# An evacuation moved ahead of the sum of the probabilities in the first stage's bodies

## What is computed

```
q = conv3x3(x, wq) + bq;  k = conv3x3(x, wk) + bk;  v = conv3x3(x, wv) + bv
bias = conv7x7(x, wb) + bb
attn = einsum('bchw,bcjw->bchj', q, k) / 16 + bias
a = softmax(attn, axis=1)                 # over the 32 channels
out = einsum('bchw,bcjw->bchj', v, a)
x = x + out
```

## Time and profile before

| | before |
|---|---|
| median of 3 runs | 1191.78 us (1188.15 to 1192.03) |
| the profiled execution: its own time | 1191.42 us |
| its span, first to last instruction | 1189.6 us |
| PE busy | 1088.5 us, 92% |
| DVE busy | 803.9 us, 68% |
| ACT busy | 536.9 us, 45% |
| POOL busy | 322.7 us, 27% |
| the line of the first stage's convolutions (L1515) on the chain that ended last | 27% |
| one turn of the loop (from 168 us on) | 73 us |

### The profile page before, as it was taken

How to read it: one execution, slowest core, us unless ns; L and a number is a source line. 1 busy time by engine, 2 the same in 40 slices (tenths; PEclk the granted TensorE clock), 3 DMA queues, 4 the chain that set the end, 5 groups by cost and what they waited for, 6 DMA issues and landing times.

```text
span 1189.6 us, 38670 instructions
## 1 busy us (share of the span) xinstructions
PE 1088.5 (92%) x17124; PEld 792.3 (67%) x17124; DVE 803.9 (68%) x994; ACT 536.9 (45%) x747; POOL 322.7 (27%) x364
## 2 busy tenths in 40 slices
PE   2999999999999999999983689887989999999997
PEld 2999999999999899999951245332434444444443
DVE  6546585685757857477297978689988645466444
ACT  3524736546364563635345857677931212111110
POOL 1374546535464363545410000023300000000000
PEclk9999999999999999999995879989999999999999
DMA  6020020200202010010002445323354654566551
GB/s 211 7 77 4 3 77 3 77 3 3 77 3 77 3 30 16 3 42 3 3 2 54 94 99 129 75 63 74 93 140 131 193 168 107 173 173 192 155 141 41
DMA packets 52116, 89.79 MB, mean 75 GB/s; under 512 B 8795, under 2 KB 36699, under 8 KB 50940
## 3 DMA queue, kind: packets, MB, share of 16 engines
q1 hardware_dynamic: 44264, 80.56, 24.5%
q10 hardware_dynamic: 7700, 6.89, 2.0%
HBM read 36.89 MB, written 11.99 MB: 41 GB/s over the span
## 4 chain that ended last, share of the span: by engine, by line
PE 62%; DVE 22%; ACT 6%; issue 4%; SPq 2%; DMA 2%; DVEq 0%; ACTq 0%
PE psum L1515 27%; PE psum L1768 15%; PE psum L1779 10%; PE psum L1668 4%; DVE small L705 3%; DVE small L672 2%; DMA arena<-arena 2%; PE psum L1570 2%; ACT arena L1206 1%; DVE arena L625 1%; DVE small L586 1%; DVE arena L1004 1%; DVE small L665 1%; DVE psum L664 1%; DVE arena L677 1%
## 5 line engine op out<-in xcount | busy, mean ns | idle before, releaser
L1515 PE MATMUL psum<-arena 128*128 128x64 f16 (+2 forms) x11904 | 511.2, 206 | 24.1 <-DMA arena<-arena 12.6
L1515 PEld LDWEIGHTS psum<-arena 128*128 128x128 f16 x11904 | 493.7, 98 | 39.9 <-DVE arena L625 13.3
L625 DVE TENSOR_TENSOR arena<-psum,arena 128x512 f32<-128x512 f32 x128 | 87.8, 690 | 169.6 <-PE psum L1515 138.4
L1768 PE MATMUL psum<-arena 128*128 128x512 f16 (+2 forms) x936 | 191.5, 365 | 0.0
L1768 PEld LDWEIGHTS psum<-arena 128*128 128x128 f16 x936 | 91.9, 98 | 98.0 <-issue 2.3
L1427 POOL TENSOR_SCALAR arena<-arena,constants_f 128x256 f16<-128x256 f16 x126 | 138.6, 1128 | 0.0
L1423 POOL TENSOR_TENSOR arena<-arena 128x256 f16<-128x256 f32 x63 | 51.4, 816 | 305.7 <-ACT arena L1185 305.7
L1779 PE MATMUL psum<-arena 120*128 120x512 f16 (+1 forms) x528 | 116.9, 379 | 0.4 <-DMA arena<-edge_columns 0.4
L1180 ACT ACTIVATE arena<-arena 128x256 f16<-128x256 f32 x63 | 26.1, 415 | 188.3 <-issue 105.3
L1779 PEld LDWEIGHTS psum<-arena 120*128 120x128 f16 (+1 forms) x528 | 51.3, 97 | 62.5 <-issue 0.9
L1471 POOL TENSOR_TENSOR arena<-arena 128x1024 f32<-128x1024 f32 x16 | 30.4, 1898 | 207.5 <-ACT arena L1327 154.6
(11 more groups left out here) (211 smaller groups left out, 1434.3 us busy)
## 6 DMA issues: line engine op xcount, KB each, us to landing
arena<-in_filter_tables SPq DMA_DIRECT2D x8, 1280.0 KB, 8.6
arena<-arena SPq DMA_DIRECT2D x32, 264.0 KB, 3.9
X<-in_x SPq DMA_DIRECT2D x16, 512.0 KB, 4.8
arena<-arena SPq DMA_DIRECT2D x32, 256.0 KB, 3.9
out<-X SPq DMA_DIRECT2D x16, 512.0 KB, 4.0
arena<-edge_columns SPq DMA_DIRECT2D x90, 80.0 KB
arena<-edge_columns ACTq DMA_DIRECT2D x70, 80.0 KB
arena<-arena SPq DMA_DIRECT2D x32, 140.0 KB, 2.6
```

The costliest lines, as they stand in the source:

```text
L625: v.tensor_tensor(out_, bank_rows(k), biasrow, ALU.add).then_inc([g.staged0, g.staged1][k], 1)
L1515: last = mm(conv[k][:, c0:c1], win[:, kk, lx, y + e, dx:dx + W, :].rearrange("p w s -> p (w s)"), wt[:, lw, d, w0:w1], start=(n == 0), sto ...
L1768: mm(bank[4 * s + 2 * f + hf][:, C * lo:C * hi], tb[:, f, d + 2, lt], xt[s][:, hf, lx, YP + d + lo:YP + d + hi].rearrange("p y c -> p (y c)"),
```

## The change

In every body, DVE's four evacuations between the sum of the probabilities and the end of the softmax move up by one softmax step. Evacuation (2, 0) now stands ahead of `softmax_sum`, (2, 1) ahead of `softmax_scale`, (3, 0) ahead of `softmax_low(j, 0)`, and (3, 1) ahead of `softmax_low(j, 1)`. Nothing is added or removed, and no other engine's program changes.

```diff
                 evacuate(i, 1, 0)
                 softmax_shift(j)
                 evacuate(i, 1, 1)
+                evacuate(i, 2, 0)
                 softmax_sum(j)
-                evacuate(i, 2, 0)
+                evacuate(i, 2, 1)
                 softmax_scale(j)
-                evacuate(i, 2, 1)
+                evacuate(i, 3, 0)
                 softmax_low(j, 0)
-                evacuate(i, 3, 0)
+                evacuate(i, 3, 1)
                 softmax_low(j, 1)
-                evacuate(i, 3, 1)
                 evacuate_rows(i, 4, 6)
                 add_attention(j, (0, 1))
```

## The result

The changed kernel takes 1180.26 us, the median of 8 runs (1177.88 to 1184.82), against 1188.74 us for the kernel before (8 runs, 1187.94 to 1192.03). The ratio is 0.9924, with a 95% interval of 0.9905 to 0.9942: 9 us faster, give or take 2 (the medians are 8.5 us apart). The forecast was 1181.3 us (1178.0 to 1185.5), for a gain of 10.5 us from the 1191.78 us that three runs of the kernel before had shown.

A forecast was written before the change was run, and what follows sets the result against it. PE was taken as the bound, waiting 11.4 us for evacuations; removing all but four waits gives 10.5 us, so the profiled 1191.42 us becomes 1180.9, plus 0.36 to the runs' median: 1181.3 us (1178.0 to 1185.5).

The forecast's parts named there:

- The order on DVE makes the waits: DVE's order alone, not its load, makes PE's waits before y2 = 3 (1.70 us) and y2 = 4 (0.37 us).
- The sum of 10.5 us: PE's removed waits: 2.07 us each in bodies 2 to 5, 1.8 in body 6, 0.39 in body 1, none in 7.
- The softmax 0.6 us late in the loop: On DVE the sum starts behind evacuation (2, 0), at 182.0 instead of 181.44; scale, halves and lows come 0.6 us later.
- The turn of the loop: One turn of the loop, from (2, 0) to (2, 0), should take 71.0 us in the changed profile.
- The tightest place inside the body: Evacuation (4, 0) would end at 203.0; PE wants its bank after attend, at 203.6: 0.6 us to spare.
- The port: SBUF port pair shared by DVE and POOL: DVE's scale may wait for POOL's L1428, softmax 0.1 to 0.2 us later still.
- The copies: Next pair's window copies would land at 229.2, PE coming at 229.46: 0.3 us to spare, and 0.26 more.
- the first rival: Copies or (4, 0) become PE's new wait, 0.3 to 1 us in bodies 2 to 6: 1183 to 1186 us; 2 in 10.
- Bodies 1 and 7 at no cost: Softmax 2.4 and 2.7 us late there, but (4, 0) keeps about 0.9 us to spare in both, so costed at nothing.
- The rival "slower": Each us chunk (2, 0) ends after the exponential delays softmax, POOL's row group 2, (4, 0) and PE; 4 in 100.
- the turning point: The change becomes a loss where the softmax comes more than 3.3 us late in bodies 2 to 5.

The follow-up runs named there:

- e6: Against the kernel before, only evacuations (3, 0) and (3, 1) moved ahead of the first and second low: 1185.97 us, ratio 0.9953, stage 3.3 us shorter.
- e2: Changed kernel with window copies of the high halves no longer waiting for `low_a`: 1175.23 us, ratio 0.9892 to the kernel before, stage 12.7 us shorter.
- e5: Changed kernel with (2, 1) also moved ahead of the sum: 1202.82 us, ratio 1.0096 to the kernel before, stage 11.0 us longer.

## Why the prediction was right, point by point

**The order on DVE makes the waits: right.** With the order changed the waits before y2 = 3 and y2 = 4 are gone in every body, and in e6 exactly the one goes whose evacuations were moved.

**The sum of 10.5 us: the mechanism right, the size too small by 2.2 us.** e2 shows what the moved evacuations are worth when nothing else stops PE: 12.7 us. The step that was mis-sized is "bodies 2 to 5: 1.70 + 0.37 = 2.07 us each". Measured from start to start it is 25.90 - 23.48 = 2.42 us. The reason can be read in the earlier trace rows: a pair of chunks is listed with 7.99 or 8.00 us, but the next row starts 7.83 us later when PE runs through. So a row's listed end lies 0.16 us behind the start of the next one, and the listed idle time, which is counted from that end, is 0.16 us less than what the wait costs from start to start. From 187.02 to 195.38 it is 8.36 us, which is 7.83 + 0.37 + 0.16; and 2 x 0.16 + 2.07 is 2.4. Body 1 gave 0.79 us for 0.39 forecast (98.05 to attend at 130.14 before, 129.35 after): 0.16 of it is the same, and the rest is a delay before y2 = 3 too short to be named.

**The softmax 0.6 us late in the loop: right.** The sum starts 0.61 us behind (2, 0), and the scale came 0.43 us later against PE. In bodies 1 and 7 the sum came 2.3 and 2.7 us later, for 2.4 and 2.7 forecast. The turn of the loop, forecast at 71.0 us, takes 70.6 us in e2; in the changed kernel it is 71.5, 74.3, 70.8 and 70.4 us from one sum to the next, bodies 2 to 6, the longest being the one with the slow clock.

**The tightest place inside the body, evacuation (4, 0), 0.6 us to spare: right.** It ended 0.6 us ahead of PE's chunk, in the changed kernel as forecast. e5, with the sum 4.5 us later than before, drove it over the edge, by 0.17 us a body.

**The port: a small price, as weighed.** POOL's last instruction of row group 1 was 0.67 us long this time:

```profile
186.15 0.67 POOL L1428 TENSOR_TENSOR arena<-arena 128x256 f32 x1
```

It started ahead of DVE's scale (186.52), which took 2.44 us instead of 2.28. Before, the scale was first and POOL took 2.79 us. So in this body the loser changed sides with the order of starting, which agrees with the Trainium skill's rule of the lock on the shared port pair (SBUF — State Buffer, "SBUF: two separate sides"). The agreement is in the sides, not in the size: the two overlapped by 0.30 us, and the scale's row is only 0.16 us longer. In the other six bodies the scale took 2.28 us, and nowhere did this bring a wait of PE.

**The copies, "0.3 us to spare, and 0.26 us more": wrong, and this is the first rival.** The rival with 2 in 10 named what happened, though its 1183 to 1186 us did not come. Two numbers of that step failed. PE comes to the copies 2.4 us sooner, not 2.07, for the same 0.16 us as above. And I took the time of the copies from one body, 6.85 us from the end of `low_a` to the landing at 229.7, as if it were the same in each. After the change it was 7.7 us in the second body (221.53 to 229.27) and 9.1 in the third (292.94 to 302.04); the last copy of the second body, on the chain of work:

```profile
225.49 3.78 DMA arena<-arena
```

The kernel before already had this spread, and the prediction did not use it. Its third body, in four rows: the end of `low_a`, the issue of the sixth copy and that copy's time to landing (the view of line L405 from 299.85 to 300.4 us), and PE's next chunk:

```profile
292.93 3.01 DVE L616 TENSOR_TENSOR arena<-arena 32x2048 f32 x1
...
L405 SPq DMA_DIRECT2D arena<-arena x1: 573/573/573, 299.9 to 299.9; - x1
...
DMA to landing us min/median/max: 4.0/4.0/4.0
...
304.59 7.99 PE L1515 MATMUL psum<-arena 128*128 128x256 f16 x186
```

The last copy landed at 303.9, 8.0 us behind `low_a` and only 0.65 us ahead of PE, where the second body had 1.8 us. By the prediction's own terms (copies 0.5 us earlier, PE 2.07 us earlier) PE would wait 0.9 us there. `low_a` itself was on time: it ended 45.0 us after PE's start on y2 = 2, 45.5 before. The rival's range, "PE waits anew 0.3 to 1 us in bodies 2 to 6", was too small as well: 1.14 and 2.31 us are over it, and it had no term for the 1.6 us of slow clock behind the longest.

**Why the total was still close.** Start to start, in the profile: 12.7 us from the moved evacuations, plus 1.2 us of waits before y2 = 2 that PE no longer showed because it was late, less 6.8 us for the copies (5.2 of waiting and 1.6 of slow clock) is 7.1 us, and the stage measured 7.2. The forecast of 10.5 us was too low in its gain and had left out this loss: two errors of opposite sign, which left it 3.3 us above the stage. That the time came within 1 us of the forecast is luck besides. The forecast started from a median of three runs, 1191.78 us; over eight runs the kernel before has 1188.74 us, and the same 10.5 us taken from that would have said 1178.2 us, at the edge of the range.

**Bodies 1 and 7 at no cost: right.** From the scores to attend body 7 took 34.19 us before (530.65 to 564.84) and 34.10 us after (523.56 to 557.66), with the softmax 2.7 us late.

**The rival "slower", each us by which an evacuation in front of the sum is late being added to the softmax: not here, but real.** e5 built that case with the sum 4.5 us late. The prediction had put the turning point at 3.3 us, and a loss of 7 us at 4.2 us late. It lost 11 us (1202.8 against 1191.7 us); the copies, for which PE waited 0.5 to 1.7 us in six bodies, are the part that the prediction had not counted.

Open: why the copies of the third body take longer than the others. Both profiles of the changed kernel show one long issue (1.59 and 1.22 us instead of 0.57) there. One thing stands beside it, a transfer on the instruction queue, here in the DMA view of the changed kernel from 295.8 to 296.2 us (packets, MB, share):

```profile
q8 instruction: 1, 0.02, 20.2%
```

It starts at 296.08, the long issue at 296.16. The eight profiles hold 288 issues of such copies in bodies 1 to 6, and 25 of them took 0.85 us or more; beside every one of the 25 such a transfer starts, at most 0.8 us before the issue or 0.1 us after it. Beside 15 issues of ordinary length there is one too, beside the other 248 none. The sixth copy of 4.0 us in the kernel before had one starting on its way as well, but so had many quick copies. No run moved these transfers, so this is a suspicion and not a shown cause.

## What to carry to other kernels

When an engine works through its instructions in order and serves two chains, what counts is not its load but what each of the consumers has to stand behind. A single piece of the fast chain moved ahead can hand the wait to the next one and lose (+4.1 us for (2, 0) alone, -12.7 us for all four, with the copies out of the way). Before costing a gain on the bounding engine, write down for every other thing that engine waits for in the turn how early it is, and take its spread over several bodies, not one: a spare of 0.3 us was not one. Copies that wait for two producers can be split so that only the second half stands behind the later one (5.5 us here, nothing where PE was not waiting).

## What the runs showed of the hardware

A wait of PE between two pairs of chunks costs its listed idle time plus 0.16 us in these traces, since a pair is listed with 7.99 us and the next row starts 7.83 us behind it when nothing is waited for.

In both profiles of the changed kernel, behind waits of 2.23 and 2.31 us, PE's granted clock was at its lower level (0.50) and 186 matmuls took 9.61 instead of 7.99 us. Behind waits of 1.70 us (the kernel before) and 1.72 us (e5) the clock was 1.00, and they took 8.00 and 7.99 us. So here the step from 1.7 to 2.3 us of waiting cost not 0.6 but 2.2 us.
